# Denominators as two extra columns of the first relational convolution's sums, exponentials written to PSUM

## The reference, cut to what matters

```
xr = einsum('nd,rdf->rnf', x, W)
oi = xr[etype, dst];  oj = xr[etype, src]
alpha = leaky_relu(oi @ q + oj @ k, 0.2)
e = exp(alpha - segment_max(alpha, dst)[dst])
z = segment_sum(e, dst)
a = e / (z[dst] + 1e-16)
out = segment_sum(a * oj, dst) + b        # per head
```

## Time and profile before

| | us |
|---|---|
| three runs | 1660.28, 1661.84, 1662.0 |
| median | 1661.84 |
| the profiled execution | 1661.59 |
| its span, first to last instruction | 1659.9 |

### The profile page before, as it was taken

The page is one execution under the profiler, slowest core; times in us unless marked ns, Lnnn a source line. Parts: engine busy times, 40 slices in busy tenths (PEclk is TensorE's granted clock), DMA queues, the critical chain, the costliest instruction groups (busy, mean ns, idle before and its releaser), DMA issues. The chain is left out here.

```text
span 1659.9 us, 23797 instructions
## 1 busy us (share of the span) xinstructions
PE 1612.4 (97%) x8691; PEld 1425.9 (86%) x8691; DVE 1060.8 (64%) x2099; ACT 696.0 (42%) x1125; POOL 648.7 (39%) x606
## 2 busy tenths in 40 slices
PE   7899999999999999999999999999999999999998
PEld 4378799999999998789988899888888888999977
DVE  8757888787887867866786467753333222444646
ACT  4334534444344435434786553433243234322231
POOL 0042152433524323237776866114343344333421
PEclk9999999999999999999999999999999999999999
DMA  4256131321313233134100323113322223323241
GB/s 128 72 182 232 30 109 54 105 77 58 115 52 101 77 115 105 34 111 142 30 1 2 120 81 105 64 55 99 94 81 80 83 80 94 91 73 106 86 143 39
DMA packets 57181, 145.38 MB, mean 88 GB/s; under 512 B 13936, under 2 KB 17136, under 8 KB 56048
## 3 DMA queue, kind: packets, MB, share of 16 engines
q1 hardware_dynamic: 50448, 111.11, 21.7%
q10 hardware_dynamic: 6624, 32.77, 5.7%
HBM read 131.80 MB, written 12.06 MB: 87 GB/s over the span
## 5 line engine op out<-in xcount | busy, mean ns | idle before, releaser
L923 POOL TENSOR_TENSOR w_pair<-early,w_pair 128x384 fp32r<-128x384 f32 x468 | 490.2, 1086 | 863.7 <-ACT w_pair L1759 863.5
L1013 PE MATMUL ps<-w_pair,cols_x 128*128 128x384 f32 x2052 | 370.2, 337 | 3.4 <-DVE al_part L2265 2.2
L1013 PEld LDWEIGHTS ps<-w_pair,cols_x 128*128 128x128 f32 x2052 | 357.9, 189 | 6.4 <-DVE al_part L2265 2.5
L1759 ACT ACTIVATE w_pair<-early 128x768 fp32r<-128x768 f32 x234 | 182.3, 839 | 302.1 <-PE ps L1013 130.0
L1013 PE MATMUL ps<-w_pair,wide 128*128 128x384 f32 x1728 | 302.3, 334 | 0.3 <-DVE early L2259 0.3
L1013 PEld LDWEIGHTS ps<-w_pair,wide 128*128 128x128 f32 x1728 | 300.1, 188 | 1.5 <-DVE early L2259 0.6
L1696 PE MATMUL ps<-wide,w_pair 128*128 128x512 f32 x972 | 228.8, 394 | 1.9 <-DVE wide L2256 1.8
L1696 PEld LDWEIGHTS ps<-wide,w_pair 128*128 128x128 f32 x972 | 182.0, 189 | 42.7 <-DVE wide L2256 4.4
L1174 PE MATMUL ps<-prob,wide 128*128 128x512 f32 x576 | 136.6, 396 | 0.4 <-DVE yt L2358 0.2
L1644 PE MATMUL ps<-prob,wide 128*128 128x512 f32 x546 | 137.0, 390 | 0.0
L1174 PEld LDWEIGHTS ps<-prob,wide 128*128 128x128 f32 x576 | 107.8, 188 | 27.3 <-issue 3.8
(11 more groups left out here) (349 smaller groups left out, 2175.6 us busy)
## 6 DMA issues: line engine op xcount, KB each, us to landing
early<-weights SPq DMA_DIRECT2D x246, 384.0 KB, 3.1
edge_mask<-counts ACTq DMA_DIRECT2D x13, 512.0 KB, 3.3
multi<-attn ACTq DMA_DIRECT2D x8, 768.0 KB, 4.4
kept<-early ACTq DMA_DIRECT2D x3, 1536.0 KB, 5.9
counts<-tally SPq DMA_DIRECT2D x12, 256.0 KB, 4.5
multi<-kept ACTq DMA_DIRECT2D x2, 1536.0 KB, 6.5
edge_mask<-masks ACTq DMA_DIRECT2D x5, 512.0 KB, 3.5
last_raw<-weights SPq DMA_DIRECT2D x6, 384.0 KB, 5.3
```

The lines of the kernel that those rows point to most:

```text
L923: return nc.gpsimd.tensor_tensor(dst, whole, high.bitcast(F32), ALU.subtract)
L1013: mm = nc.tensor.matmul(ps[:, m, 0:HW], left[:, a, k, m * P:(m + 1) * P], w_pair[:, slot_of[0], b, k, :], start=(k == 0 and a + b == 0), s ...
L1759: return nc.scalar.activation(dst, src, ACT.Copy)
```

## The change

- **Ones between the heads' features.** A row block's half of 384 columns (two heads) is kept as 192 columns, two columns of ones, 192 columns. The even head of the pair is multiplied as its 192 columns and the ones, the odd one as the ones and its 192 columns: 194 columns in both products with the high features. The product with the low features stays at 192. The denominators come out as columns beside the sums, and the products with the matrix of ones are gone. ACT writes the two columns for each of the 24 tiles. One of the eight halves of a relation lies in a new tensor `row_ends`, over part of `early`.
- **Exponentials in PSUM.** `exp_tile` writes to banks 4 and 5, which are free now, and `weigh` reads from there.
- **u and v inside products.** The transposes and spreads are issued between the chunks of products 16, 17, 21 and 22, three pairs of spreads instead of two before the loop; ACT takes exponentials from product 16 on, and the table of the exponential is loaded at product 13. The high part of pass 37 is split in three. In the loop `copy_v1` comes after tile 4j's high part, not after tile 4j - 1's.
- **Buffers and the tail.** The last head has its own buffers (`homes`). Pass 39's split, the DMA issues and POOL's subtractions for pass 39 come before the last head's steps, and the last head is turned after 18 products of pass 38, not 24.

```diff
+        def half_block(r, m, n):
+            if (m, n) == (NB - 1, 1):
+                at = 2 * D + r * (HALF + 2)
+                return row_ends[:, at:at + HALF + 2]
+            at = (2 * m + n) * HALF
+            return wide[r][:, 0, at:at + HALF + 2]
...
+            weights_low(1, 3 * 39)
+            pool.wait_ge(w_low, 3 * 40)
             piece_low(HEADS1 - 1, 0)
             piece_low(HEADS1 - 1, 1)
-            weights_low(1, 3 * 39)
-            pool.wait_ge(w_low, 3 * 40)
...
+            within = {16: {1: turn_all_uv, 4: spread_first_v}, 17: {1: spread_first_u, 4: lambda: spread_u(1)},
+                      21: {4: lambda: spread_v(2)}, 22: {3: lambda: spread_u(2)}}
...
-                    for a in range(2):
-                        nc.tensor.matmul(ps[:, 4 + h % 2, :], ones[:], prob[:, a, s, :], start=(begin and a == 0), stop=(end and a == 1))
+                    led = h % 2
+                    with_ones = half_block(r, s, h // 2)[:, led * SHARE:(led + 1) * SHARE + 2]
                     for m in range(NB):
-                        for a, b in ((0, 0), (0, 1), (1, 0)):
-                            mm = nc.tensor.matmul(ps[:, 2 * (h % 2) + m // 2, m % 2 * SHARE:(m % 2 + 1) * SHARE],
-                                                  prob[:, b, s, m * P:(m + 1) * P], rows[r][:, a, s, h * SHARE:(h + 1) * SHARE],
-                                                  start=(begin and a + b == 0 and m % 2 == 0), stop=(end and a == 1), skip_group_check=True)
+                        bank, at = 2 * (h % 2) + m // 2, m % 2 * (SHARE + 2)
+                        for b in range(2):
+                            nc.tensor.matmul(ps[:, bank, at:at + SHARE + 2], prob[:, b, s, m * P:(m + 1) * P], with_ones,
+                                             start=(begin and b == 0 and m % 2 == 0), stop=False, skip_group_check=True)
+                        mm = nc.tensor.matmul(ps[:, bank, at + 2 * led:at + 2 * led + SHARE], prob[:, 0, s, m * P:(m + 1) * P],
+                                              rows[r][:, 1, s, h * SHARE:(h + 1) * SHARE], start=False, stop=end, skip_group_check=True)
...
-            first_product(38, (0, 1), range(4))
+            first_product(38, (0, 1), range(3))
             turn_head(HEADS1 - 1, 6)
+            first_product(38, (0, 1), range(3, 4))
...
             def exp_tile(k):
                 h, s = k // TILES, k % TILES
-                exponential(W_AT + k, k % 2, ks1[:, 1, s // 4, h, s % 4:s % 4 + 1], counts_for(k))
+                act.wait_ge(x_pre, W_AT + k + 1)
+                nc.scalar.activation(ps[:, 4 + k % 2, :], xt[:, k % 2], ACT.Exp,
+                                     bias=ks1[:, 1, s // 4, h, s % 4:s % 4 + 1]).then_inc(x_exp, counts_for(k))
...
-                if s % 4 == 3 and k // 4 + 2 < REL3 * HEADS1:
-                    copy_v1(k // 4 + 2)
+                if k > 4 and k % 4 == 0 and k // 4 + 1 < REL3 * HEADS1:
+                    copy_v1(k // 4 + 1)
...
-                    copy_tile(32 + 2 * r + n, m, n, 64 + t, rows[r], lows=t, dots_done=64)
+                    if t == 15:
+                        act.wait_ge(max_done, 17)
+                    copy(half_block(r, m, n)[:, SHARE:SHARE + 2], ones[:, 0:2].bitcast(F32))
+                    copy_tile(32 + 2 * r + n, m, n, 64 + t, None, lows=t, dots_done=64)
+                    if 17 <= t < 21:
+                        high_tile(t - 17)
+                    if t >= 17:
+                        exp_tile(t - 15)
...
+            split_high(39, 1)
+            act.wait_ge(x_lo, W_AT + HEADS1 * TILES)
+            act.dma_start(acc[:, 0:2], attn2.partition_broadcast(P)).then_inc(vec_in, 16)
+            act.dma_start(mask[:], masks[1]).then_inc(mask_in, 16)
             scale_head(HEADS1 - 1, range(NB))
...
-                for m in range(NB):
-                    mark(nc.vector.tensor_tensor_reduce(out=r_den[:, m * P:(m + 1) * P], in0=ps[:, 4 + h % 2, m * P:(m + 1) * P],
-                                                        in1=ident[:], scale=1.0, scalar=EPS_SOFTMAX, op0=ALU.mult, op1=ALU.add,
-                                                        accum_out=columns[:, m:m + 1]))
+                banks = ps[:, 2 * (h % 2):2 * (h % 2) + 2, 0:2 * (SHARE + 2)].rearrange("p b (k c) -> p b k c", k=2)
+                mark(nc.vector.tensor_scalar(columns.rearrange("p (b k) -> p b k", b=2), banks[:, :, :, 0 if h % 2 else SHARE],
+                                             EPS_SOFTMAX, None, ALU.add))
```

More of the change, by code:

```diff
@@ L52, in early_loads @@
 def early_loads(nc, ctx):
+    with nc.sbuf_tensor("row_ends", [P, 2 * D + REL3 * (HALF + 2)], F32R) as row_ends:
+        pass
     early = ctx.enter_context(nc.sbuf_tensor("early", [P, NB * D + 8 * HW], F32))
@@ L622 @@
 SHARE = D // HEADS1
+HALF = 2 * SHARE + 2
 def tile_at(h, s):
@@ L665, in graph_layers @@
             pass
+        with nc.sbuf_tensor("prob_scratch", [P, 2 * NB * N], F32) as prob_scratch:
+            pass
         prob = sb("prob", [P, 2, NB, N], F32R)
@@ L1472, in _ @@
                     elif t >= NB:
-                        product(32 + 2 * r + n, m, cols_x, tile_copied, 64 + 8 * r + 4 * n - 4 + m + 1)
+                        product(32 + 2 * r + n, m, cols_x, tile_copied, 64 + 8 * r + 4 * n - 4 + m + 1, inside=within.get(t, {}))
                     if t == 2:
@@ L1498, in turn_head @@
                     for m in range(NB):
-                        mm = nc.tensor.transpose(ps[0:end - begin, bank + c, m * P:(m + 1) * P], head_rows[:, m, begin:end], ident[:])
+                        mm = nc.tensor.transpose(ps[0:end - begin, bank + c, m * P:(m + 1) * P], head_rows[h // (HEADS1 - 1)][:, m, begin:end], ident[:])
                     mm.then_inc(head_turned, 1)
@@ L1512, in _ @@
                 for s in range(NB):
-                    if s == 1 and g + 2 < rounds:
+                    if s == 1 and 0 < g < rounds - 2:
                         spread_v(g + 2)
-                    elif s == 2 and g + 2 < rounds:
+                    elif s == 2 and 0 < g < rounds - 2:
                         spread_u(g + 2)
@@ L1759, in copy, with split_part @@
                 return nc.scalar.activation(dst, src, ACT.Copy)
+            def split_part(j, slot, p, wait=True):
+                act.wait_ge(raw_in[p], j * 16 + 16)
+                if p == 0 and wait:
+                    act.wait_ge(prod_done, j * 4 - 4)
+                copy(w_pair[:, slot, 0, 2 * p:2 * p + 2, :], w_raw[:, p]).then_inc(w_high, 1)
             def split_high(j, slot, wait=True):
                 for p in range(3):
-                    act.wait_ge(raw_in[p], j * 16 + 16)
-                    if p == 0 and wait:
-                        act.wait_ge(prod_done, j * 4 - 4)
-                    copy(w_pair[:, slot, 0, 2 * p:2 * p + 2, :], w_raw[:, p]).then_inc(w_high, 1)
+                    split_part(j, slot, p, wait)
             def copy_tile(j, m, n, q, dst, first=False, lows=None, dots_done=None, direct=False):
@@ L1819, in piece_exponent @@
                 act.wait_ge(head_turned, 2 * h + c + 1)
-                nc.scalar.activation(piece_exp[c][part], ps[part, bank + c, :], ACT.Exp, bias=bias).then_inc(elu_parts, 1)
+                nc.scalar.activation(piece_exp[h // (HEADS1 - 1)][c][part], ps[part, bank + c, :], ACT.Exp, bias=bias).then_inc(elu_parts, 1)
             def piece_sum(h, c, bank):
@@ L1827, in piece_sum @@
                     act.wait_ge(piece_lo, 2 * (h - 1) + c + 1)
-                nc.scalar.activation(piece_out[c][part], ps[part, bank + c, :], ACT.Identity, bias=bias)
+                nc.scalar.activation(piece_out[h // (HEADS1 - 1)][c][part], ps[part, bank + c, :], ACT.Identity, bias=bias)
             def piece_relu(h, c):
@@ L1833, in piece_relu @@
                 act.wait_ge(elu_parts, 2 * (2 * h + c) + 1)
-                nc.scalar.activation(piece_exp[c][part], piece_exp[c][part], ACT.Relu, bias=1.0, scale=-1.0).then_inc(elu_parts, 1)
+                nc.scalar.activation(piece_exp[h // (HEADS1 - 1)][c][part], piece_exp[h // (HEADS1 - 1)][c][part], ACT.Relu, bias=1.0, scale=-1.0).then_inc(elu_parts, 1)
             def piece_high(h, c):
@@ L1839, in piece_high @@
                 act.wait_ge(agg_read, 48 + 2 * h + c + 1)
-                copy(cols_x[part, 0, f, :], piece_out[c][part]).then_inc(piece_hi, 1)
+                copy(cols_x[part, 0, f, :], piece_out[h // (HEADS1 - 1)][c][part]).then_inc(piece_hi, 1)
             def high(w, y, dst, part=slice(0, P), by=1):
@@ L2343, in exponent, with weigh @@
                 nc.vector.scalar_tensor_tensor(xt[:, slot], u, source, v, ALU.add, ALU.max).then_inc(x_pre, by)
-            def weigh(w, slot, y, count, before=None, by=1):
+            def weigh(w, slot, y, count, before=None, by=1, source=None):
                 dve.wait_ge(x_exp, w + 1)
```

91 lines of the change are left out of this document (53 added, 38 removed).

## The result

The changed kernel takes 1638.38 us (median of 4 runs, 1637.64 to 1639.46), the kernel before 1661.92 on the same chip: a ratio of 0.986, 95% interval 0.9845 to 0.9875. That is 23.5 us less, where 26.9 were forecast. 1638.4 lies in the range and 3.4 us over the point. The profiled execution took 1637.64 us, with a span of 1635.9.

A forecast was written before the change was run, and what follows sets the result against it. TensorE was busiest in the heads' loop, with VectorE and ACT close behind and VectorE and POOL stretching each other. Gains of 22.3 (loop), 3.1 (tail) and 1.5 us (clock) sum to 26.9: forecast 1635 us, range 1629 to 1646.

The forecast's parts named there:

- Loop entry: Start of the heads' loop: 0.7 us later, at 803.75, for moved transposes, two more spreads and a wait for v2.
- 194 columns: TensorE's products in the loop: growing from 192 to 194 columns costs 0.3 us in all, a tile taking 1.32 us.
- Rival 3: TensorE's loop: 194 columns fall off the fast form; slower past 0.09 us extra, 1679 at 512-column price; chance 0.05.
- Exponentials in PSUM: VectorE and POOL in the loop: `weigh` falls from 1.04 to 0.70 us, POOL's subtraction to 1.28 plus 0.07 wait.
- rival 2: Loop: VectorE and POOL still stretch each other despite the PSUM source; loop 85, gain 18.7 us, kernel 1643; chance 0.14.
- ACT overlaps its starts: ACT in the loop: operations start before the last one ends, so a tile takes 1.13 us, not 1.34.
- Rival 1: Loop: ACT does not overlap its own starts; loop 89.6 us, gain 14.3, kernel 1647; chance 0.14.
- The loop: Summing of the heads: ACT bounds heads 1 to 3, loop 78.5 us, end at 882.2 against 904.55, gain 22.3 us.
- for waits that four coupled queues leave: Loop: an allowance of 1.8 us added to the heads' sum of 76.7 us.
- Tail: Loop's end to the next product: 14.1 us instead of 17.2, by moving pass 39's work ahead; gain 3.1 us.
- Clock behind the tail: 922 to 927 us: the granted clock's dip to 0.66 goes as the 2.2 us stall shrinks; gain 1.5 us.
- Rival 4: Loop: nothing happens, TensorE's saving returns as waits for ACT's later v copies; kernel 1660; chance 0.04.

The follow-up runs named there:

- e2: Changed kernel with the exponentials written to SBUF again and read there by `weigh`: 1647.68 us, ratio 0.9917 to the kernel before.
- e7: Changed kernel with 18 unread products of 124 columns issued ahead of each of TensorE's two long waits for v: 1638.52 us, ratio 0.9862 to the kernel before.
- e9: Changed kernel with POOL's last low part of the last head ahead of a piece of the head before: 1638.32 us, ratio 0.9861 to the kernel before.
- e1: Changed kernel with ACT's copy of v back behind tile 4j - 1: 1640.41 us, ratio 0.987 to the kernel before.
- e5: Changed kernel with the four scalings of a head on VectorE instead of ACT: 1639.57 us, ratio 0.9877 to the kernel before.
- e10: Changed kernel with u's spread one tile later, at step 3 of its group instead of 2: 1639.04 us, ratio 0.9861 to the kernel before.
- e4: Changed kernel with the tail's order as before, head turned after 24 products: 1644.42 us, ratio 0.9899 to the kernel before.
- e3: Kernel before with 88 of the 96 products with ones left out, nothing else changed: 1660.59 us, ratio 0.9997 to the kernel before.
- e8: Changed kernel without the head start of transposes, spreads and exponentials, v copies behind tiles 4j - 1: 1640.64 us, ratio 0.9875 to the kernel before.
- e0: Changed kernel run again without an edit, in another session: 1637.75 us, ratio 0.9857 to the kernel before.

## Why the prediction was right, and where it was off

- **Loop entry.** Held: 0.04 us later than before. It was forecast as 0.7 later, but TensorE was already 0.7 us earlier in this execution before the first moved step (the last spread of the relations starts at 766.41 against 767.10), so the step's own 0.7 is there. The first exponential's table load moved to 770.86 us, where ACT has idle time.
- **194 columns.** Held. Three products, 194, 194 and 192 columns, take 0.33 us, so each spaces at 0.11 us and a tile takes 1.34 us against 1.32:

```profile
808.11 0.39 PE L1547 MATMUL ps<-wide,prob 128*128 128x194 f32 x2
808.33 0.27 PE L1549 MATMUL ps<-wide,prob 128*128 128x192 f32 x1
808.44 0.39 PE L1547 MATMUL ps<-wide,prob 128*128 128x194 f32 x2
```

Rival 3 is excluded by these lines.

- **Exponentials in PSUM.** Held, and e2 shows it as the cause: 686 ns against 700 forecast for `weigh`, 1289 against 1280 for POOL, so rival 2 is out. ACT's exponential got shorter too, 690 ns against 721, with starts still 0.61 us before the next operation's. The rule of the Trainium skill, "SBUF — State Buffer", Who interferes with whom, agrees with the change and with its undoing in e2. The Trainium skill's "VectorE: DVE Perf Modes", the TRN2 errata, gives a PSUM source some 60 cycles more; that is not to be seen in this operation, whose shortest `weigh` takes 673 ns with a source in PSUM and 677 ns in the kernel before with both in SBUF.
- **ACT overlaps its starts.** Held: 837.28, 837.80 and 838.27 are starts of a copy, a v copy and an exponential, 0.52 and 0.47 us apart at durations of 0.61 and 0.57. Rival 1, with full durations, would have made the loop 89.6 us.
- **The loop: the mis-sized term.** 78.5 us were forecast and 83.6 came. The mechanism was right: after head 0 ACT is the bound, at 20.74 of 21 us. By heads the loop took some 17.0, 22.5, 24.3 and 19.8 us where 16.8, 20.7, 20.7 and 18.5 were summed, so most of the excess is in head 2, where the sign "ACT idle under 5%" failed (19.71 of 22 us). The term that failed is the 1.8 us "for waits that four coupled queues leave"; it measured 6.9. The sentence "TensorE waits for them at every fourth tile, but it has slack there" failed with it: TensorE had slack for a wait, but not for the half clock behind it, which holds up ACT in turn. Of the missing 5.1 us, the clock took 1.6 to 2.2 (e7) and POOL's piece ahead of the last low part 0.9 to 1.5 (e9). Some 1.4 to 2.6 are left, which are put down to the hand-offs between ACT and the others by what remains, not by a run. The runs e1, e5 and e10 each change which engine waits for which and shorten nothing; they do not divide the rest further.
- **Tail.** Held: 14.1 us as forecast, gain 3.0 against 3.1. TensorE's 54 products run without a stall, and POOL's work for pass 39 runs from 886.72, as the loop ends, to 892.57, before the first piece is wanted (893.93). e4 confirms it.
- **Clock behind the tail.** Held: the granted clock in 922 to 927 is 1.00 instead of 0.66, and the 126 products take 1.6 us less, against 1.5. It came back in e4 with the old tail; in e3, which has the old tail and a stall of 2.02 us, it did not come, so it is not certain to follow the stall. A second 1.5 us came from a dip further on in the profile of before that this profile lacks (54 products in 12.4 instead of 13.9 us). It was not in the sum, and is chance: e3 lacks it with the kernel before's code there, and e4 and e7 have it with the changed kernel's. Without it the gain would be 22.4 us.
- **Rival 4.** Wrong of the whole change. The removal of the ones products alone has its outcome (e3), for another reason.

In the sum: 17.8 for the loop and its entry instead of 22.3, 3.0 for the tail, 1.6 for the clock and 1.5 by chance make 23.9, the difference of the two profiled executions (23.95).

## What to carry to other kernels

When four engines are close to each other, taking 21 us of work from the one at the bound can be worth next to nothing until the next one is relieved as well (e3: 2.0 us of loop, whole time unchanged; the whole change: 23.5 us, of which undoing the PSUM exponentials alone costs 9.3 and undoing the tail alone 6.0). Price the stretching of one engine by another as its own term, and read it from the same operation with and without the neighbour. Add to the balance of a loop not only waits but what they do to TensorE's clock, and expect that moving one late step in the middle of such a loop moves the wait, not the end (e1, e5, e10); at the loop's end it can count (e9). Before a run is read as the price of one step, look for another run that shares a part of its edit: e8 looked like the price of the head start until e1 stood beside it.

## What the runs showed of the hardware

- Behind idle stretches of 2.17 and 2.82 us TensorE ran at 0.52 and 0.50 of its full clock for 3 us and more; in other runs such stretches lasted 6 to 7 us (e0: 0.50 and 0.51 in 863 to 869; e8: 0.62 on average in the 9 us from 839 to 848). It does not follow each time: in e0 the clock stayed at 1.00 behind the first of the two, and in the kernel before behind a wait of 2.05 us. Nor does it need a wait of 2 us: in e10 it came after waits of 0.63 and 0.87 us and during one of 1.21. With products in place of the idle time there was no dip in the loop (e7).
- An exponential of 512 columns from SBUF takes 690 ns into PSUM and 721 to 727 into SBUF.
- VectorE's operation of two 512-column sources takes 686 ns with one of them in PSUM and 973 to 1064 with both in SBUF while POOL subtracts, and POOL's subtraction 1289 ns against 1532 to 1585.
